# Casts of the line coordinates moved to ScalarE, the first tile's slots filled in parts, and a decoder layer's order of work chosen anew

## The chip, the cores and the metric

One core of a Trainium2 chip. The metric is the device time of one execution in microseconds (us). The engines are named as in the profile: PE (TensorE, matrix products), PEld (its weight loads), DVE (VectorE), ACT (ScalarE), POOL (GpSimd), SP (SyncE, which here only starts transfers).

## The reference

One decoder layer on x of 2048 tokens by 256, in float32:

1. `x = x + attn(layernorm(x))`. Self attention with 16 heads, causal, of an unusual kind. Of each token and head two 4-vectors `q1, q2` are made from the token and its predecessor, and two, `k1, k2`, from the token. Each pair becomes a line of 6 coordinates, `p1[i]*p2[j] - p1[j]*p2[i]` over the 6 pairs of indices, divided by its norm. Logits are products of the lines of queries and keys, times 6^-0.5.
2. `x = x + xattn(layernorm(x), ctx)`. Cross attention, 16 heads, over a context of 1601 rows.
3. `x = x + ffn(layernorm(x))`. 16 experts, 64 tokens each, chosen with 6 Sinkhorn rounds and a top-k, hidden width 1024.

## The kernel before

**Tiles.** The tokens are cut into 4 tiles of 512 (`NT`), each of 4 blocks of 128 (`BPT`). Self attention runs over query tiles, 4 groups of 4 heads, and key blocks up to the diagonal; cross attention over query tiles, groups and 13 context blocks. One block of one group is a *quad*: 160 of self attention and 208 of cross attention, 368 in all. A quad is two `scores` steps (products of keys and queries into one of two PSUM pairs, then one exponential on ACT, L1216, into `probs`; on the diagonal POOL then masks, L1076) and one `pv` step (the product with the values into `po`, L1824). At the end of a group ACT copies `po` out (L1228).

**Lines.** The 6 coordinates of a tile's queries and keys are made on DVE in steps `("lines", j, part)`. Part 0 (L1415 to L1421) makes the products, part 1 (L1425 to L1429 and `rsqrt`, L1280 to L1285) their difference and its inverse norm. Part 2 (L1438 to L1442) multiplies by it and cuts each float32 into three bfloat16 parts, so that bfloat16 products keep the precision:

```
l3 = l3 * rn
line_parts[0] = bf16(l2)                 # cast, L1439
t2 = l2 - line_parts[0]                  # L1440
line_parts[1] = bf16(t2)                 # cast, L1441
line_parts[2] = t2 - line_parts[1]       # L1442
```

For a product six combinations of the parts of a query and a key are stacked as six *slots*: `Q_SLOTS = (0, 1, 0, 1, 2, 0)`, `K_SLOTS = (0, 0, 1, 1, 0, 2)`. For tiles 1 to 3 the parts are turned by PE (`line_turn`, L1900), stored to DRAM and loaded into the slots by 24 transfers. The first tile takes a shorter way: `("slots", 0)` copies the parts into `slotted` with `copy_to_slots` (L839), the 12 copies of the queries on ACT and the 12 of the keys on DVE, both after L1442; then 8 `slot_turn` steps, each 8 transposes on PE (L1889) and a copy of the result by ACT (L1156) or DVE, fill `q_line` and `k_line`. The first scores (L1804) wait for all 8.

**Around them.** `prep` steps load and normalize the tokens (`stats` L1293, `norm` L1367, `x_turn` L1867) and `project` them (L1877, L1880; the result copied out at L1394 and L1396 by DVE, or L1151 and L1153 by ACT). `ctx_k` (L1852) and `ctx_v` (L1861) project the context, `join` adds an attention's result, `max` steps (L1932 on PE, L1509 on DVE: 64 for each of 16 tile-groups) find the largest cross logit of each token and head. A `shift` step and `shift_turn` (L1517 to L1529) turn the maxima of one tile-group into a row that is stored (L966), loaded (L972) and subtracted in the cross scores; without it the scores of that tile-group can't begin.

**The order.** Every engine is in order, and all take their instructions from one list, `PLAN`. `build_plan` makes it: ten streams of steps (`x`, `lines`, `ctx`, `keys`, `ones`, `max`, `query`, `weights`, `scores`, `pv`) are merged greedily. Each candidate step costs its idle time and start, and for each other stream the delay it causes there times a weight of that stream (table `W`). The durations and waits that the planner assumes stand in `work()`. The streams `lines`, `ctx` and `x` have weights of their own (`early_...`) until tile 1's lines are loaded. The weight of `max` is `W["max"]` while `max` steps lag behind `(pv steps done - max_from) / (368 - max_end - max_from)` of them, else `max_ahead`. The planner also chooses, for the kinds in `EITHER`, whether DVE or ACT copies a result out of PSUM; `act_early` and `act_late` are what ACT costs extra before and after the first scores.

## Time and profile before

| | us |
|---|---|
| median of 3 runs (lowest, highest) | 1152.06 (1151.38, 1155.24) |
| the profiled execution's own time | 1152.26 |
| its span | 1150.5 |
| PE busy | 1096.7 (95%) |
| DVE busy | 853.2 (74%) |
| ACT busy | 725.3 (63%) |
| POOL busy | 142.1 (12%) |

The span is what the profiler saw between the first and the last instruction; 1.76 us of the execution's own time lie around it. The granted PE clock is shown in tenths of full speed in the page's slices, and as a fraction in the table of stretches. Busy time of PE is modelled from pipelined records, so a PE at 95% is not at 95% of its peak; what counts below is where it is idle, and at which clock it works.

### The profile page before, as it was taken

How to read it: one execution, taken by the hardware profiler on the slowest of the kernel's cores; microseconds unless marked ns; L12 is line 12 of the kernel's file. 1: busy time of each engine (PE TensorE's matmuls, PEld its weight loads, DVE VectorE, ACT ScalarE, POOL GpSimd, SP SyncE). 2: the span in 40 equal slices, each digit the busy share in tenths (PEclk: the TensorE clock that was granted, in tenths of full speed). 3: DMA queues.
4: the chain of work that ended last, by engine and by line, in shares of the span. 5: the costliest groups of instructions: out<-in, count | busy, mean ns of one | idle time of the engine just before them, and what ended most of it. 6: DMA issues, size and time to landing. Idle time of an engine off the chain costs nothing.

```text
span 1150.5 us, 30375 instructions
## 1 busy us (share of the span) xinstructions
PE 1096.7 (95%) x12606; PEld 512.7 (45%) x12606; DVE 853.2 (74%) x1999; ACT 725.3 (63%) x838; POOL 142.1 (12%) x253
## 2 busy tenths in 40 slices
PE   4799999999999999999999999999999999888997
PEld 2444332333433334444455555555555553467554
DVE  6965676288889898789888889788888892258621
ACT  0646577887677776776776787678785778520111
POOL 3142314122111101000101000010000000000222
PEclk8899999999999999999999999999999999889999
DMA  5031037932100100103321200111102000088696
GB/s 177 27 82 55 24 108 127 177 59 69 44 30 2 47 16 16 53 19 87 121 70 59 94 19 23 53 48 31 30 10 73 21 17 3 19 296 217 185 349 180
DMA packets 79241, 90.24 MB, mean 78 GB/s; under 512 B 16016, under 2 KB 71632, under 8 KB 79104
## 3 DMA queue, kind: packets, MB, share of 16 engines
q1 hardware_dynamic: 73200, 79.91, 24.5%
q10 hardware_dynamic: 4368, 6.29, 1.7%
q0 software_dynamic: 1536, 2.10, 1.0%
q8 instruction: 100, 1.64, 0.6%
q14 instruction: 37, 0.30, 0.1%
HBM read 73.36 MB, written 14.91 MB: 77 GB/s over the span
## 4 chain that ended last, share of the span: by engine, by line
PE 84%; DVE 8%; ACT 3%; issue 3%; POOL 1%; DMA 0%; DVEq 0%; POOLq 0%; ACTq 0%
PE po L1824 25%; PE g L1932 17%; PE scores L1800 15%; PE scores L1804 6%; PE g L1917 3%; PE g L2029 2%; PE g L2053 2%; PE g L1877 2%; ACT probs L1216 2%; PE g L1907 2%; PE g L1867 1%; PE g L1923 1%; PE g L1911 1%; PE g L1852 1%; PE scores L2042 1%
## 5 line engine op out<-in xcount | busy, mean ns | idle before, releaser
L1216 ACT ACTIVATE probs<-scores 128x1024 f32<-128x1024 f32 (+2 forms) x736 | 675.3, 967 | 236.8 <-PE scores L1800 132.3
L1509 DVE TENSOR_REDUCE mx<-g 128x1 f32<-128x400 f32 (+1 forms) x1024 | 524.2, 567 | 74.0 <-PE g L1932 64.6
L1932 PE MATMUL g<-cross_region,even_region 96*32 96x400 bf16 (+1 forms) x4096 | 306.0, 336 | 0.4
L1800 PE MATMUL scores<-even_region,cross_region 99*32 99x512 bf16 (+1 forms) x3264 | 252.2, 379 | 2.5 <-ACT probs L1216 2.5
L1824 PE MATMUL po<-probs,cross_region 128*32 128x512 f32 (+1 forms) x1664 | 223.4, 594 | 0.8 <-ACT probs L1216 0.8
L1932 PEld LDWEIGHTS g<-cross_region,even_region 96*32 96x32 bf16 x4096 | 120.0, 95 | 196.6 <-DVE mx L1509 99.4
L1824 PE MATMUL po<-probs,self_region 128*32 128x512 f32 (+3 forms) x1280 | 151.3, 547 | 3.3 <-POOL probs L1076 3.0
L1800 PEld LDWEIGHTS scores<-even_region,cross_region 99*32 99x32 bf16 (+1 forms) x3264 | 96.5, 96 | 98.2 <-issue 43.2
L1804 PE MATMUL scores<-self_region 36*128 36x512 bf16 (+3 forms) x640 | 103.4, 358 | 6.2 <-ACT probs L1216 4.2
L1043 POOL TENSOR_TENSOR rstd<-mv,half 128x1 f32<-128x1 f32 x48 | 28.0, 584 | 529.5 <-DVE mv L1295 529.5
L1076 POOL TENSOR_SCALAR_AFFINE_SELECT probs<-probs 128x256 f32<-128x256 f32 x128 | 56.7, 449 | 231.8 <-ACT probs L1216 230.9
L1804 PEld LDWEIGHTS scores<-self_region 36*128 36x128 bf16 x640 | 25.7, 93 | 118.1 <-ACT probs L1216 82.5
L1824 PEld LDWEIGHTS po<-probs,cross_region 128*32 128x32 f32 (+1 forms) x1664 | 55.2, 110 | 25.7 <-ACT probs L1216 5.9
L1246 ACT ACTIVATE even_region<-scores 128x1024 f32<-128x1024 f32 x4 | 4.1, 1023 | 81.8 <-PE scores L2042 81.8
L1833 PE MATMUL scores<-xbo_sb,ident 128*128 128x256 f32 x186 | 47.3, 406 | 0.0
L1824 PEld LDWEIGHTS po<-probs,self_region 128*32 128x32 f32 x1280 | 31.6, 110 | 31.0 <-issue 15.3
L1483 DVE RECIPROCAL rsum<-g 128x16 f32<-128x16 f32 x32 | 8.2, 256 | 47.5 <-PE g L1907 47.3
L1867 PE MATMUL g<-ident,xn 128*128 128x128 f32 x96 | 21.5, 307 | 18.9 <-DVE xn L1367 18.7
L1833 PEld LDWEIGHTS scores<-xbo_sb,ident 128*128 128x128 f32 x186 | 36.6, 203 | 5.3 <-issue 0.3
L1877 PE MATMUL g<-wself_sb,xn_t 128*128 128x512 f32 x64 | 34.0, 658 | 0.0
L1494 DVE TENSOR_TENSOR xb<-g,xb 128x256 f32<-128x256 f32 x32 | 13.6, 424 | 24.3 <-PE g L1917 23.6
L1228 ACT COPY o_region<-po 128x512 f32<-128x512 f32 x32 | 18.8, 588 | 14.0 <-PE po L1824 14.0
(294 smaller groups left out, 863.8 us busy)
## 6 DMA issues: line engine op xcount, KB each, us to landing
cross_region<-in_w SPq DMA_DIRECT2D x16, 1024.0 KB, 12.7
even_region<-xq_d SPq DMA_DIRECT2D x192, 64.0 KB, 2.3
self_region<-in_w ACTq DMA_DIRECT2D x6, 1024.0 KB, 6.6
self_region<-in_w SPq DMA_DIRECT2D x6, 1024.0 KB, 14.6
cross_region<-xk_d SPq DMA_DIRECT2D x24, 200.1 KB, 8.8
xb<-in_x SPq DMA_DIRECT2D x32, 128.0 KB, 3.2
xb<-x_d SPq DMA_DIRECT2D x32, 128.0 KB, 2.3
probs<-in_w SPq DMA_DIRECT2D x4, 1024.0 KB, 12.6
```

Of the source, the lines that this page charges most:

```text
L1043: pool.tensor_tensor(rstd[:, u % 4:u % 4 + 1], mv[:, u % 4, 1:2], half[:, 0:1], ALU.pow).then_inc(rstd_ready, 1)
L1076: pool.affine_select(out=d, in_=d, compare_op=ALU.is_ge, fill=0.0, base=0, pattern=[[0, 2], [1, P]], channel_multiplier=-1).then_inc(mask_ ...
L1216: act.activation(probs[0:rows, s % 4, :, off:], ps[s % 2][0:rows, :, off:], ACT.Exp, scale=LSCALE if QUADS[n][0] == "self" else 1.0).then_ ...
L1509: dve.reduce_max(mx[:, k % 2, b, h, c:c + 1], g[:, 0:n_keys], AX_X).then_inc(g_free, 1)
L1800: mm = pe.matmul(ps[s % 2][c:c + n_keys, a, :], k_cross[0:NS * DH + 3, h, i * P + c:i * P + c + n_keys], rhs, start=True, stop=True)
L1804: mm = pe.matmul(ps[s % 2][0:rows, a, off:], lhs, rhs, start=True, stop=True)
L1824: mm = pe.matmul(po[32 * a:32 * a + 32, off:], v[0:rows, i, h * VW:h * VW + 32], probs[0:rows, s % 4, a % 2, off:], start=(i == 0), stop=e ...
L1833: pe.matmul(bank, ident[:, :], xbo_sb[:, :], start=True, stop=True)
L1867: mm = pe.transpose(g[:, k * P:(k + 1) * P], xn[:, norm_no[u] % 2, k * P:(k + 1) * P], ident[:, :])
L1877: pe.matmul(g[:, :], xn_t[:, k, c + 1:c + 1 + P], wself_sb[:, k, 0:512], start=(k == 0), stop=False)
L1917: mm = pe.matmul(g[:, 0:D], attn_t[:, k, :], (wo_sb if step[1] == "self" else wxo_sb)[:, k, :], start=(k == 0), stop=(k == DK - 1))
L1932: mm = pe.matmul(g[q:q + 32, 0:n_keys], q_max[k % 2][0:NS * DH, h, b * P + q:b * P + q + 32], k_cross[0:NS * DH, 4 * (k % 4) + h, start:st ...
```

## The change

It does three things.

1. **Casts.** Part 2 of `lines` becomes parts 2, 3 and 4. DVE multiplies and signals `lines_whole`; ACT makes the first cast and signals `lines_cast`; DVE subtracts (part 3); ACT makes the second cast; DVE subtracts the last time (part 4). The instructions of part 0 move into a helper, `line_products`, unchanged.
2. **Slots.** `copy_to_slots` takes the part that it is to copy. `("slots", 0)` and `("slots", 1)` copy the slots that hold part 0 and part 1 (3 and 2 of the six, 6 and 4 copies on either engine) as soon as ACT has cast them, `("slots", 2)` the last one (2 copies). On DVE the order is part 3, slots 0, part 4, slots 1, slots 2; on ACT cast, cast, slots 0, slots 1, slots 2.
3. **Order.** Fifteen weights of the planner are different, and its table of durations has the new steps, so the whole list is another.

```diff
-W = dict(hungry=0.2496, fed=0.0083, act_near=0.2255, max=0.1307, max_ahead=0.0147, max_from=72.59, max_end=10.0224,
-         prep=0.7203, x=0.2428, lines=0.1574, ctx=0.1821, keys=0.0826, early_ctx=0.1984, early_lines=7.9028,
-         early_x=0.84, ones=0.4536, query=0.3458, weights=0.0036, start=0.5141, late=0.9255, act_late=70.0,
+W = dict(hungry=0.2498, fed=0.0083, act_near=0.2255, max=0.4357, max_ahead=0.0147, max_from=72.59, max_end=3.5078,
+         prep=0.1816, x=0.2428, lines=0.1873, ctx=0.1393, keys=0.0688, early_ctx=0.8164, early_lines=3.9514,
+         early_x=1.372, ones=0.4083, query=1.1524, weights=0.005, start=0.7342, late=0.9255, act_late=35.7,
          act_early=0.0026)
...
-        line_steps += [("lines", j, part) for part in range(3)]
+        line_steps += [("lines", j, part) for part in range(4)]
         if j == 0:
-            line_steps += [("slots", j)] + [("slot_turn", b, side) for b in range(BPT) for side in range(2)]
+            line_steps += [("slots", 0), ("lines", 0, 4), ("slots", 1), ("slots", 2)]
+            line_steps += [("slot_turn", b, side) for b in range(BPT) for side in range(2)]
             continue
+        line_steps += [("lines", j, 4)]
...
-            return [("DVE", (3.7, 6.8, 5.0)[part], before, step, LAG)]
+            if part == 0:
...
+                return [("DVE", 3.6, before, step, LAG)]
+            if part == 1:
+                return [("DVE", 6.8, [("lines", j, 0)], step, LAG)]
+            if part == 4:
+                return [("DVE", 1.0, [("lines_cast", j, 3)], step, LAG)]
...
+            return [("DVE", 1.0, before, step, LAG), ("ACT", 0.75, [step], ("lines_cast", j, part), LAG)]
         if kind == "slots":
-            return [("ACT", 4.3, [("lines", 0, 2)], ("slots_q",), LAG), ("DVE", 2.7, [("lines", 0, 2)], step, LAG)]
+            part = step[1]
+            before = [("lines_cast", 0, part + 2) if part < 2 else ("lines", 0, 4)]
+            return [("ACT", 0.72 * (3 - part), before, ("slots_q", part), LAG),
+                    ("DVE", 0.45 * (3 - part), before, step, LAG)]
...
-        def copy_to_slots(copy, side):
+        def copy_to_slots(copy, side, which):
 
             for s, part in enumerate((Q_SLOTS, K_SLOTS)[side]):
+                if part != which:
+                    continue
...
# ScalarE
-                elif step == ("slots", 0):
-                    act.wait_ge(lines_split, 1)
-                    last = copy_to_slots(act.copy, 0)
-                    last.then_inc(slots_q, 1)
+                elif step[0] == "lines" and step[2] in (2, 3):
+                    _, j, part = step
+                    act.wait_ge(lines_whole, 2 * j + part - 1)
+                    src = (lines if part == 2 else lines_t).rearrange("p s h c -> p s (h c)")
+                    act.copy(line_parts[:, :, part - 2, :], src).then_inc(lines_cast, 1)
+                elif step[0] == "slots":
+                    if step[1] < 2:
+                        act.wait_ge(lines_cast, step[1] + 1)
+                        copy_to_slots(act.copy, 0, step[1])
+                    else:
+                        act.wait_ge(lines_split, 1)
+                        copy_to_slots(act.copy, 0, 2).then_inc(slots_q, 1)
...
# VectorE
-                        link(dve.tensor_tensor(l3, l3, line_rn.unsqueeze(2).broadcast_to((P, 8 * H, NC)), ALU.mult))
-                        link(dve.tensor_copy(line_parts[:, :, 0, :], l2))
-                        link(dve.tensor_tensor(t2, l2, line_parts[:, :, 0, :], ALU.subtract))
-                        link(dve.tensor_copy(line_parts[:, :, 1, :], t2))
+                        dve.tensor_tensor(l3, l3, line_rn.unsqueeze(2).broadcast_to((P, 8 * H, NC)),
+                                          ALU.mult).then_inc(lines_whole, 1)
+                    elif part == 3:
+                        dve.wait_ge(lines_whole, 2 * j + 1)
+                        dve.wait_ge(lines_cast, 2 * j + 1)
+                        dve.tensor_tensor(t2, l2, line_parts[:, :, 0, :], ALU.subtract).then_inc(lines_whole, 1)
+                    else:
+                        dve.wait_ge(lines_whole, 2 * j + 2)
+                        dve.wait_ge(lines_cast, 2 * j + 2)
                         dve.tensor_tensor(line_parts[:, :, 2, :], t2, line_parts[:, :, 1, :],
                                           ALU.subtract).then_inc(lines_split, 1)
                 elif kind == "slots":
-                    dve.wait_ge(lines_split, 1)
-                    copy_to_slots(dve.tensor_copy, 1).then_inc(slots_k, 1)
+                    if step[1] < 2:
+                        dve.wait_ge(lines_cast, step[1] + 1)
+                        copy_to_slots(dve.tensor_copy, 1, step[1])
+                    else:
+                        dve.wait_ge(lines_split, 1)
+                        copy_to_slots(dve.tensor_copy, 1, 2).then_inc(slots_k, 1)
```

## Rows read from the trace of the kernel before

**Rows 1.** The page's head, and its slices of PE busy and PE clock over the span
```profile
span 1150.5 us, 30375 instructions
...
PE   4799999999999999999999999999999999888997
PEclk8899999999999999999999999999999999889999
```

**Rows 2.** Busy time of each engine in stretches between events: us (instructions), clock, DMA share, GB/s
```profile
20.80:35.60 14.80, 7.91 (x22) 4.35 (x22) 13.93 (x49) 2.24 (x7) 2.49 (x4) 0.65 0.10 28
35.60:44.60 9.00, 7.35 (x27) 4.09 (x28) 7.41 (x22) 4.77 (x18) 0.00 (x0) 1.00 0.06 15
44.60:52.70 8.10, 5.18 (x68) 4.07 (x69) 7.79 (x29) 7.47 (x9) 1.09 (x2) 1.00 0.15 51
52.70:60.00 7.30, 6.07 (x32) 0.97 (x32) 6.75 (x17) 4.80 (x8) 3.18 (x6) 0.53 0.00 0
100.00:320.00 220.00, 213.10 (x1810) 77.01 (x1809) 148.15 (x348) 156.92 (x187) 50.68 (x93) 0.98 0.38 83
957.50:993.00 35.50, 31.85 (x407) 10.13 (x404) 1.02 (x4) 33.28 (x36) 0.00 (x0) 1.00 0.01 2
```

**Rows 3.** The timeline, 20 to 33 us: start, duration, engine, line, operation, idle before
```profile
24.38 0.43 DVE L1293 BATCH_NORM_STATS2 bn<-xb 128x6 f32<-128x256 f32 x1
26.64 0.66 PE L1867 MATMUL g<-ident,xn 128*128 128x128 f32 x2 [6.93 <-DVE xn L1367]
28.21 3.62 PE L1877 MATMUL g<-wself_sb,xn_t 128*128 128x512 f32 x4
32.67 1.88 PE L1877 MATMUL g<-wself_sb,xn_t 128*128 128x512 f32 x4
```

**Rows 4.** The timeline of VectorE, part 2 of the first tile's lines
```profile
35.65 0.95 DVE L1438 TENSOR_TENSOR even_region<-even_region 128x768 f32<-128x768 f32 x1
36.63 0.56 DVE L1439 CAST even_region<-even_region 128x768 bf16<-128x768 f32 x1
...
38.82 0.96 DVE L1442 TENSOR_TENSOR even_region<-even_region 128x768 bf16<-128x768 f32 x1
```

**Rows 5.** The timeline, first tile's slots, turns and first scores
```profile
39.89 1.54 DVE L839 COPY probs<-even_region 128x192 bf16<-128x192 bf16 x12
40.92 0.38 ACT L1153 COPY even_region<-g 128x256 f32<-128x256 f32 x1
41.18 3.13 ACT L839 COPY probs<-even_region 128x192 bf16<-128x192 bf16 x12
45.23 7.41 ACT L1156 COPY self_region<-g 100x1024 bf16<-100x1024 bf16 x8 [0.91 <-PE g L1889]
52.69 0.86 PE L1804 MATMUL scores<-self_region 36*128 36x512 bf16 x4 [1.39 <-ACT self_region L1156]
```

**Rows 6.** ScalarE's groups nearest to the new cast, from the page and from one line's durations
```profile
L1216 ACT ACTIVATE probs<-scores 128x1024 f32<-128x1024 f32 (+2 forms) x736 | 675.3, 967 | 236.8 <-PE scores L1800 132.3
L1228 ACT COPY o_region<-po 128x512 f32<-128x512 f32 x32 | 18.8, 588 | 14.0 <-PE po L1824 14.0
...
L1156 ACT COPY self_region<-g x8: 1012/1042/1077, 45.2 to 51.6; 100x1024 bf16<-100x1024 bf16 x8
```

**Rows 7.** The timeline around the last tile's second cast
```profile
182.23 1.43 POOL L1068 MEMSET cross_region<- 32x1604 f32 x1 [2.48 <-DMA xk_d<-cross_region]
182.31 1.77 DVE L1441 CAST even_region<-even_region 128x768 bf16<-128x768 f32 x1
184.38 0.42 PE L1824 MATMUL po<-probs,self_region 128*32 128x128 f32 x8 [1.67 <-POOL probs L1076]
```

**Rows 8.** The end of the maxima: their line, the last shift's load, the last group's first scores
```profile
L1509 DVE TENSOR_REDUCE mx<-g x28: 560/566/575, 939.5 to 956.0; 128x1 f32<-128x400 f32 x21, 128x1 f32<-128x401 f32 x7
...
960.25 0.25 SPq L972 DMA_DIRECT2D even_region<-shift_d  x1
965.74 0.61 PE L1800 MATMUL scores<-even_region,cross_region 99*32 99x512 bf16 x8
```

More of the change, by code:

```diff
@@ L285, in work @@
             b = step[1]
[L286 removed]
+            return [("PE", 0.5, [("lines", b // BPT, 4)] + bank, ("line_turn_pe", b), LAG),
                     (by, 0.8 if by == "ACT" else 0.57, [("line_turn_pe", b), ("line_stored", b - 4)], ("line_turn", b), LAG),
@@ L1430, in _ @@
                         rsqrt(line_rn, line_n2, flat_t[:, 0:P])
-                    else:
+                    elif part == 2:
                         if j == 1:
```

44 lines of the change are left out of this document (24 added, 20 removed).

## The prediction

> **What bounds the kernel now.** I first read the page's head and slices [rows 1]: PE is busy nine tenths or more nearly everywhere, and its clock is full except in a few slices. The whole is bound by PE, so a change gains only where PE is idle or at its lower clock. Then I cut the span at events [rows 2]. Four places are open. From 20.8 to 35.6 us PE works 7.91 of 14.80 us, at a clock of 0.65, while DVE is busy 13.93. From 44.6 to 52.7 PE works 5.18 of 8.10 while ACT is busy 7.47. From 52.7 to 60 PE works 6.07 of 7.30 at a clock of 0.53. From 100 to 320 it is idle 220.00 - 213.10 = 6.90 us. The fifth, 957.5 to 993, has ACT at 33.28 of 35.50: there the exponentials set the pace.
>
> Up to the first scores at 52.69 [rows 5] one chain matters: projections, lines on DVE, slots, turns. The timeline shows its end. DVE multiplies at 35.65, casts, subtracts, casts, subtracts until 38.82 + 0.96 = 39.78 [rows 4]. ACT, held until 41.30 by a copy of a projection, makes its 12 slot copies from 41.18 to 44.31; DVE's 12 take 1.54 and end at 41.43. Then ACT alone empties the eight turns, 7.41 us from 45.23 [rows 5]. What feeds PE other work in that time comes late: it is idle 6.93 us before the transposes at 26.64, since DVE makes part 0 of the lines and then, from 24.38, the statistics that the normalization waits for [rows 3].
>
> **The casts.** A cast of 768 elements takes DVE 0.56 [rows 4]. ACT's is not in the trace: a copy of 512 takes 0.588, one of 1024 two-byte elements 1.042 [rows 6]; midway is 0.81, and I take 0.80, with the two rows as bounds. Each cast also has two hand-offs. On DVE the first slot copy follows the last subtraction by 39.89 - 39.78 = 0.11, and ACT's copies of even 0.38 overlap, 41.18 being before 40.92 + 0.38 [rows 4, 5]; I take 0.05 for each. The pitch of DVE's cast is 0.60: from 36.63 to 38.82 lie two casts and a subtraction, and the multiplication, as long as a subtraction, has a pitch of 36.63 - 35.65 = 0.98 [rows 4], so (2.19 - 0.98) / 2. Part 2 then ends 2 x (0.80 + 0.10 - 0.60) = 0.6 later than 39.78, at 40.4.
>
> The Trainium skill has a rule against this, in "ScalarE: Activation LUTs", section "Rules for kernel authors": plain arithmetic belongs on VectorE, which is faster per element. Its own figure, 186 ns plus 0.833 per element, gives an estimate of 0.83 us for this cast, and so 0.06 more for the pair than my sum; the row of DVE agrees that VectorE is faster here.
>
> **The slots.** ACT's pitch is 3.13 / 12 = 0.26 [rows 5]. Its queue is cast, cast, then 6 + 4 copies from about 39.4, which end at 42.0, then the last 2, which wait for 40.4 only: 42.5, against 44.31. That is 1.8 earlier if no copy of a projection is in front, and 1.1 if a projection's two copies, of 0.38 each like the row's, still are. I take 1.3, bounds 0 and 1.8. On DVE the 6 + 4 + 2 copies end by 41.3 and don't matter.
>
> **The turns.** Eight turns cost ACT 7.41, PE only 5.18 in that stretch with all else [rows 2, 5]. Shared by DVE and ACT they could end 7.41 - 5.18 = 2.2 sooner. Weight `early_lines` halves, so DVE is less reserved for tile 1's lines, but nothing says that the planner shares them: 0.7, bounds 0 and 2.2.
>
> **The first hole.** `early_ctx` rises from 0.198 to 0.816, `early_x` from 0.84 to 1.372, and `early_lines` falls from 7.90 to 3.95. A delay of the lines was worth 40 of the context's and is now worth 5; so some context or token work should come before or between the parts of the lines, and enter PE's 6.93 us. It also delays the lines themselves. The four matrix products after the hole take 3.62 at the low clock, 1.88 later [rows 3], 1.7 more to have. Bounds 0 and 6.9 + 1.7 = 8.6. I take 2.3, near the lower end, because DVE, full at 13.93 of 14.80 [rows 2], is what context work needs too.
>
> **Later tiles.** ACT gets 6 more casts, 4.8 us, in stretches where it is busy 156.92 of 220 [rows 2], so they lie beside PE's work. DVE loses 6 x 0.6 = 3.6 us but now stands in its queue for each cast, behind at worst one exponential of 0.97 [rows 6] and with its own evacuations behind it, for which PE's three banks wait. Six times (0.97 + 0.30) = 7.6 of DVE, of which PE feels what its filler work doesn't cover: I take 0.7 lost, bounds 0 and 4.
>
> In the last tile the second cast took 1.77 instead of 0.56, overlapping a POOL memset, and PE then waited 1.67 for a mask behind it [rows 7]. With the cast on ACT, or the order another, this may go: I take 0.9 gained, bounds 0 and 1.67. The Trainium skill explains the row in "SBUF — State Buffer", section "SBUF: two separate sides": VectorE and GpSimd lock a pair of ports against each other and ScalarE has its own. By that rule an ACT cast is never held so.
>
> **Everything else** that the new order moves (weights `prep`, `query`, `ctx`, `keys`; the loads in SP's queue; the fills and masks in POOL's) goes at 0, bounds +4 and -3: it acts inside the 6.90 us idle of 100 to 320, and from 320 on PE is full [rows 1, 2]. Every instruction of PE stays, only its place changes.
>
> **Sum.** -1.3 - 0.7 - 2.3 + 0.7 - 0.9 = -4.5. The profiled execution took 1152.26, 0.20 above the median of 1152.06; so 1152.06 - 4.5 = 1147.6, call it 1147.5, which is 0.4% less. About 0.3%, 3.5 us, is what a measurement of this kernel can tell from no change: faster is below 1148.6, slower above 1155.5.
>
> **Rivals.**
>
> *The hole is filled.* Context work enters the first hole in earnest. For it: the weight ratio falls eightfold, and PE is idle there with ACT doing 2.24 of 14.80 us [rows 2]. Against: the context's cut needs DVE. Near the bounds, -1.8 - 2.2 - 6 - 1 = -11: 1141.
>
> *Given back.* First scores come earlier, but into the stretch where exponentials, masks and tile 1's lines already leave PE at a clock of 0.53 [rows 2]; an earlier start only lengthens it, as the next tile's lines are then what is late, now with two hand-offs more. For it: DVE is the fuller engine there, 6.75 of 7.30. Time 1152, or 1150 to 1154. That the change does not do what it says is part of this: the list may come out so that a projection's copies stand before the slots as now. The ScalarE page's rule of the Trainium skill points the same way.
>
> *The maxima come late* (slower). `max_end` falls from 10.02 to 3.51. When the last group of 13 quads is due, at pv 355, the wanted share is (355 - 72.59) / (368 - 72.59 - 3.51) = 0.967, before 0.990: of 1072 steps 35 may be undone, before 11. The 24 between would take DVE 24 x 0.566 = 13.6 us [rows 8]. Before, the last load of a shift was issued at 960.25, and the first scores of the last group ran at 965.74 [rows 8]: with some 2.3 for landing, as the planner takes it, 3.2 of slack. So it decides from 6 maxima more on, and at 24 costs 10.4: with the other terms 1152.1 - 4.5 + 10.4 = 1158. Against: the last maxima ran at 956.0 [rows 8], all done before the share asked for them, since PE takes them when ACT has work in store, and `max` weighs three times more when behind.
>
> **Chances.** The forecast's own case 0.38 (1143 to 1148.6), the filled hole 0.13, given back 0.31, maxima late 0.12, the waits for ACT's casts at their upper bound with nothing won 0.06. Faster 0.51, same 0.31, slower 0.18. The likeliest case alone has 1143 to 1150. The range reaches down to 1140, nearly all of the filled hole, and up to 1156, given back with its bounds and half of the slower cases.
>
> **What would show it.** Right: casts on ACT of 0.75 to 0.85; the last slot copy on ACT 0.5 to 0.7 after the last subtraction; first L1804 near 49 to 51; PE idle under 5 us before the second tile's transposes; the last tile's second cast under 1 us. Wrong: first scores at 52 or later; more idle of PE between 52 and 100 us than now; L1509 after 960 us, with PE idle in front of the last group; DVE idle behind casts on ACT for over 1 us each in 100 to 320 with PE idle beside it.

## The result, and the profile after

The kernel after the change took 1158.33 us in the median of 17 executions (1154.36 to 1163.03), the one before, run beside it on the same chips, 1151.58 (1147.93 to 1155.24, 17 executions). The ratio is 1.0058, 95% interval [1.0045, 1.0071]: 6.7 us slower, where 4.5 less was forecast, and above the range.

The page of the kernel after, its head and busy shares:

```profile
span 1155.2 us, 30383 instructions
...
PE 1096.9 (95%) x12606; PEld 512.8 (44%) x12606; DVE 850.1 (74%) x1992; ACT 729.6 (63%) x845; POOL 142.2 (12%) x253
```

PE is busy 1096.9 us, as much as before (1096.7), and the span is 1155.2 instead of 1150.5. So the 4.7 us that the profiled execution lost are idle PE; its busy time did not grow. The stretches say where (busy us of PE, PEld, DVE, ACT and POOL with their instructions, granted clock, DMA share, GB/s):

```profile
20.00:55.70 35.70, 26.23 (x136) 17.20 (x136) 31.13 (x102) 14.23 (x33) 4.69 (x8) 0.86 0.11 39
...
60.00:100.00 40.00, 36.16 (x265) 15.34 (x258) 29.94 (x68) 21.00 (x34) 17.67 (x34) 0.97 0.22 59
100.00:320.00 220.00, 211.99 (x1745) 76.13 (x1747) 134.55 (x321) 156.48 (x188) 47.85 (x91) 0.95 0.39 85
320.00:940.00 620.00, 616.74 (x8853) 285.23 (x8848) 537.03 (x1170) 462.21 (x494) 37.20 (x70) 1.00 0.15 43
...
80.00:100.00 20.00, 17.36 (x121) 7.34 (x120) 17.25 (x40) 8.88 (x15) 9.33 (x17) 1.00 0.27 75
...
160.00:180.00 20.00, 17.48 (x110) 4.44 (x110) 14.75 (x47) 13.31 (x18) 12.68 (x17) 0.74 0.91 118
```

The first row ends at the first scores, 55.70, which before came at 52.69 [rows 5]: 3.0 late. From 60 to 320 PE is idle 3.84 + 8.01 = 11.85 us. Before, it was 1.09 from 60 to 100 (busy 38.91) and 6.90 from 100 to 320 [rows 2], 7.99 in all; the clock of the longer stretch was 0.98 and is 0.95. From 320 to 940 there is 3.26 of idle PE, before 1.90 (busy 618.10), at a full clock in both. The twelfth group of heads ends at 296.57 us, before at 290.72: 5.9 late, more than the 4.8 at the end of the last group (998.87 and 994.08). So the time is lost ahead of 320 us, while the lines of the later tiles are made. The last two rows are the worst stretches of 20 us in there, with 2.64 and 2.52 of idle PE; before they had 0.13 and 0.06 (busy 19.87 and 19.94).

The first tile, in the timeline (start, duration, engine, line, operation, idle before and its releaser):

```profile
23.07 0.66 PE L1904 MATMUL g<-ident,xn 128*128 128x128 f32 x2 [3.56 <-DVE xn L1408]
...
37.36 0.95 DVE L1466 TENSOR_TENSOR even_region<-even_region 128x768 f32<-128x768 f32 x1
...
38.34 0.83 ACT L1238 CAST even_region<-even_region 128x768 bf16<-128x768 f32 x1 [1.60 <-DVE even_region L1466]
...
40.48 0.41 PE L1904 MATMUL g<-ident,xn 128*128 128x128 f32 x2 [3.56 <-DVE xn L1408]
...
41.23 0.83 ACT L1238 CAST even_region<-even_region 128x768 bf16<-128x768 f32 x1 [2.06 <-DVE even_region L1471]
...
42.24 3.15 ACT L855 COPY probs<-even_region 128x192 bf16<-128x192 bf16 x12
...
45.89 0.61 PE L1926 MATMUL g<-identb,probs 128*100 128x128 bf16 x8
...
48.48 2.30 PE L1926 MATMUL g<-identb,probs 128*100 128x128 bf16 x24 [1.99 <-DVE rest L1345]
...
52.93 1.89 DVE L1487 COPY self_region<-g 100x1024 bf16<-100x1024 bf16 x3
...
53.83 1.95 PE L1898 MATMUL g<-cross_region 128*128 128x256 f32 x8
...
55.70 0.60 PE L1841 MATMUL scores<-self_region 36*128 36x512 bf16 x4
```

Against [rows 3 to 5]: PE's one idle time of 6.93 has become two of 3.56, before different tokens' transposes. The casts on ACT take 0.83. From the multiplication to the last slot copy are 42.24 + 3.15 - 37.36 = 8.03 us, before 44.31 - 35.65 = 8.66 [rows 4, 5], so the slots did gain 0.6; but the multiplication is 1.7 later. The turns began at 45.89 and stopped for a context step (PE waits 1.99 for DVE's L1345, which frees a PSUM bank). DVE copied three of the eight results (L1487), and a context step (53.83 to 55.8) still stood ahead of the first scores.

The casts of ScalarE alone, from one line's view, and the last tile's second cast in the timeline:

```profile
L1238 ACT CAST even_region<-even_region x8: 822/832/855, 38.3 to 186.8; 128x768 bf16<-128x768 f32 x8
```

```profile
185.65 1.16 DVE L1471 TENSOR_TENSOR even_region<-even_region 128x768 f32<-128x768 f32 x1
...
186.84 0.83 ACT L1238 CAST even_region<-even_region 128x768 bf16<-128x768 f32 x1 [0.66 <-DVE even_region L1471]
```

Eight casts, 822 to 855 ns. In the last tile the cast starts 0.03 after the subtraction and takes 0.83, where DVE took 1.77 beside a memset of POOL [rows 7]; in this order no memset runs beside it. An exponential stands right behind it (187.58), but PE has a query projection to do until 187.9 and does not wait here. Nor do casts of the other tiles lie in the two worst stretches: they begin at 66.71, 69.88, 105.51 and 111.65, and ACT stood idle 0.62 ahead of the second and 2.29 ahead of the third. From this trace alone the casts look harmless, which the experiments contradict.

The end of the maxima, which one rival rested on:

```profile
L1546 DVE TENSOR_REDUCE mx<-g x1024: 552/565/578, 233.3 to 960.6; 128x1 f32<-128x401 f32 x86, 128x1 f32<-128x400 f32 x85
```

```profile
965.08 0.25 SPq L1005 DMA_DIRECT2D even_region<-shift_d  x1
...
970.54 0.61 PE L1837 MATMUL scores<-even_region,cross_region 99*32 99x512 bf16 x8
```

The last maxima begin at 960.6, the last shift's row is loaded from 965.08 and the last group's first scores run at 970.54: each 4.6 to 4.8 later than in [rows 8], and no more apart. The lateness is inherited.

### The profile page after: what moved, and what is told of

The parts are those of the page before. It is cut to its first block, busy times and chain, and to the rows that moved or that the text cites. A ratio compares the mean times of both kernels' runs of the same rounds, so it can differ in the third digit from the quotient of the medians.

```text
span 1155.2 us, 30383 instructions
## 1 busy us (share of the span) xinstructions
PE 1096.9 (95%) x12606; PEld 512.8 (44%) x12606; DVE 850.1 (74%) x1992; ACT 729.6 (63%) x845; POOL 142.2 (12%) x253
## 4 chain that ended last, share of the span: by engine, by line
PE 83%; DVE 8%; ACT 4%; issue 3%; POOL 1%; DMA 0%; DVEq 0%; POOLq 0%; ACTq 0%
PE po L1861 24%; PE g L1969 17%; PE scores L1837 15%; PE scores L1841 6%; ACT probs L1257 3%; PE g L1914 3%; PE g L1954 3%; PE g L2066 2%; PE g L2090 2%; PE g L1904 2%; PE g L1944 1%; PE scores L1870 1%; PE g L1960 1%; PE g L1948 1%; PE scores L2079 1%
## 5 line engine op out<-in xcount | busy, mean ns | idle before, releaser
L1969 PE MATMUL g<-cross_region,even_region 96*32 96x400 bf16 (+1 forms) x4096 | 309.7, 336 | 0.4
L1861 PEld LDWEIGHTS po<-probs,cross_region 128*32 128x32 f32 (+1 forms) x1664 | 55.8, 110 | 24.8 <-ACT probs L1257 4.6
```

Source lines behind the costliest of these rows:

```text
L1861: mm = pe.matmul(po[32 * a:32 * a + 32, off:], v[0:rows, i, h * VW:h * VW + 32], probs[0:rows, s % 4, a % 2, off:], start=(i == 0), stop=e ...
L1969: mm = pe.matmul(g[q:q + 32, 0:n_keys], q_max[k % 2][0:NS * DH, h, b * P + q:b * P + q + 32], k_cross[0:NS * DH, 4 * (k % 4) + h, start:st ...
```

## Experiments

Each text set off below was written before its run. Theory A, after this result: **the casts on ScalarE cost it**, through ACT's order (the second cast waits for DVE's subtraction, and exponentials queue behind). Rival B: **the new list costs it** (first scores 3 us late, turns interrupted). Rival C: both are small and the rest is the planner's luck: any list made anew lands some us away. Ratios are to the kernel before, run in the same job, with 95% intervals; a ratio of 0.001 is 1.15 us. Where an edit keeps a list (the order of work) and changes only code, this is said.

### Code against list

The list of the kernel before with the code of the change: `build_plan` as before, each old step replaced by the new ones in place.

```diff
+SPLIT = {("lines", j, 2): [("lines", j, 2), ("lines", j, 3), ("lines", j, 4)] for j in range(1, NT)}
+SPLIT["lines", 0, 2] = [("lines", 0, 2), ("lines", 0, 3), ("slots", 0), ("lines", 0, 4), ("slots", 1), ("slots", 2)]
+SPLIT["slots", 0] = []
...
-        plan.append(step)
+        plan += SPLIT.get(step, [step])
```

> The casts on ScalarE and the slots in parts, in the list of the kernel before: wherever that list had part 2 of the lines, it now has parts 2, 3 and 4 in a row, the first tile's with the slots between them; no other step moves. Theory 'order' (the new list loses the time, the casts don't): 0.997 to 1.001 of the kernel before, first scores 1 to 2 us earlier than 52.69. Theory 'hand-off' (VectorE waiting for ScalarE's casts holds PSUM banks, and PE with them): 1.003 to 1.006, with VectorE idle over 1 us in front of the subtractions of tiles 1 to 3 and PE idle beside it.

Measured: **1.0041 [1.0018, 1.0064]**, 1155.52 us. The new code alone, in the old order, costs most of the loss: theory 'hand-off' has its range, theory 'order' not. Its first scores come at 54.71, not earlier than 52.69: ACT's first cast stood behind a projection's copies, and DVE waited 3.37 us for it.

The changed kernel's list with both casts of every tile back on DVE:

```diff
-                        dve.tensor_tensor(l3, l3, line_rn.unsqueeze(2).broadcast_to((P, 8 * H, NC)),
-                                          ALU.mult).then_inc(lines_whole, 1)
+                        link(dve.tensor_tensor(l3, l3, line_rn.unsqueeze(2).broadcast_to((P, 8 * H, NC)), ALU.mult))
+                        dve.tensor_copy(line_parts[:, :, 0, :], l2).then_inc(lines_cast, 1)
```

> The changed kernel's list to the step, slots in parts too, but each cast made by VectorE inside its step, so that ScalarE has none of the 8. Theory 'order': 1.004 to 1.008 of the kernel before, as the changed kernel. Theory 'hand-off': 0.998 to 1.002, the loss is gone.

Measured: **1.0020 [1.0000, 1.0041]**, 1153.81 us, though its first scores come no earlier (56.17). So the casts are worth 0.0038 in this list (the two intervals don't meet), and the list about 0.002 without them. Its trace has the same two worst stretches, PE busy 17.98 from 80 to 100 and 17.84 from 160 to 180: these belong to the list and not to the casts. DVE is at 15.94 of 20 in the first of them, POOL at 12.99 in the second, before at 14.80 and 3.32.

The changed kernel with the weights of before, so a third list:

```diff
-W = dict(hungry=0.2498, ..., max=0.4357, ..., early_ctx=0.8164, early_lines=3.9514, early_x=1.372, ...
+W = dict(hungry=0.2496, ..., max=0.1307, ..., early_ctx=0.1984, early_lines=7.9028, early_x=0.84, ...
```

> The changed kernel with the fifteen weights of before; the planner has the new steps and makes a list of its own. Theory 'order', in the form that the weights are at fault: 0.998 to 1.003. Theory 'hand-off': 1.003 to 1.007. If any list that the planner makes is off by several us by chance, both are missed and it can lie anywhere in 0.997 to 1.008.

Measured: **1.0082 [1.0057, 1.0107]**, 1160.0 us, the slowest median of all (6 executions), with the first scores at 52.58. It is above the range of both theories; only the third, a list that is off by chance, reaches it. The weights of the change look better for the new steps than the old ones, but the intervals of 1.0058 and 1.0082 overlap. And the kernel before with the new weights (the same lines exchanged, in the kernel before), a fourth list:

> The kernel before with the fifteen new weights and nothing else. Theory 'order', weights at fault: 1.003 to 1.008. Theory 'hand-off': 0.998 to 1.002. With this and the run with the old weights the two factors, code and weights, stand crossed.

Measured: **1.0008 [0.9993, 1.0024]**, 1151.72 us. This one matters for how to read a trace. Its first group ends (ACT's copy of `po`) at 71.25 us, in the kernel before at 62.42; yet it isn't told apart from it. PE was busy 43.46 us of the first 60, before 38.4: the other work was done first. How early the first scores run says little about the end. Of the theories, A has 0.0038 of 0.0058 in one list and 0.0041 in the other; B has some 0.002; C is true of lists in general (1.0008, 1.0020 with DVE's casts, 1.0082), but doesn't explain a loss that appears with the list unchanged.

### Which tiles' casts, which part of the code

The changed kernel with ACT's casts in the first tile only, and in the later tiles only; the others' casts go back to DVE. The first of the two (the second has `step[1] > 0` and `j > 0`):

```diff
+                elif step[0] == "lines" and step[2] in (2, 3) and not (step[1] == 0):
+                    pass
...
+                        if not (j == 0):
+                            dve.wait_ge(lines_whole, 2 * j + 1)
+                            dve.tensor_copy(line_parts[:, :, 0, :], l2).then_inc(lines_cast, 1)
```

> The changed kernel's list, casts on ScalarE in the first tile only; tiles 1 to 3 cast on VectorE in the same step. With all casts on VectorE this list gave 1.002, with all on ScalarE 1.006. Theory 'later tiles' (VectorE waits for ScalarE among the exponentials): 1.001 to 1.003 here. Theory 'first tile' (the way to the first scores is what counts): 1.004 to 1.007.

> The mirror of the run before: casts on ScalarE in tiles 1 to 3, on VectorE in the first. Theory 'later tiles': 1.004 to 1.007. Theory 'first tile': 1.001 to 1.003. If the two runs both lie near 1.004, each part carries half.

Measured: 1.0065 [1.0045, 1.0085] and 1.0049 [1.0026, 1.0071]. They don't add up to the 1.0058 of both, from 1.0020 for neither: within the intervals either alone may cost as much as the two together. Theory 'later tiles' missed with the first of the two, theory 'first tile' with the second. In this list it stays open which tile's casts matter.

The traces don't settle it either. The last group ends at 997.27 us with all casts on DVE, 998.87 with all on ACT, 999.74 and 999.61 with a part of them there. What differs is the granted clock of the executions: 0.979 in the mean for the changed kernel's 17, 0.984 for the 12 with all casts on DVE. Within each of the two kernels 0.001 of clock goes with some 0.8 to 1.0 us, so these 0.005 are an estimate of 4 to 5 us, as much as the 0.0038. So in this list the price of the casts goes with PE's clock. That the casts lower it, by holes behind which the clock falls, fits the pair below, but isn't shown here.

The old list (`SPLIT` as in the first experiment), the slots in parts, all casts on DVE; and the same with the casts of tiles 1 to 3 on ACT. Between the two stands only

```diff
-                        if not (j > NT):
+                        if not (j > 0):
                             dve.wait_ge(lines_whole, 2 * j + 1)
```

and its like for the second cast and on ACT.

> The list of the kernel before, all casts on VectorE, only the first tile's slots in parts (part 3 between, the project copy and the carry after the slots). If this part of the change is worth what I gave it, ScalarE ends its slot copies 1 to 2 us earlier than 44.31, first scores come near 51, and the ratio is 0.997 to 1.000. If filling in parts is what loses (its copies stand in front of other steps): 1.002 or more.

> As the run before, with the casts of tiles 1 to 3 on ScalarE. Against that run it measures the hand-off in the later tiles alone, in the old list, in which VectorE's step was never planned with a wait: theory 'later tiles' 0.002 to 0.005 more than the run before; theory 'first tile' no more than 0.001 more, and then the 1.004 of the old list with all casts on ScalarE is owed to the first tile's cast, which stood 3.37 us behind two copies of a projection.

Measured: **0.9989 [0.9972, 1.0006]**, 1149.68 us, and **1.0048 [1.0030, 1.0067]**, 1156.98 us. Here is the clean pair: one list, six casts moved, 0.0059, a little more than theory 'later tiles' allowed. The ends of groups in the two traces are the same within 1.7 us up to the seventh (after the first, 1.5 apart; after the seventh, 1.6); the eighth ends at 185.75 in the one and at 191.34 in the other, the last at 995.18 and 1001.61. So 5.6 of 6.4 us are there by 191, and 4.0 of them came between the ends of the seventh group and the eighth, while the lines of tile 3 are cut. The timelines there, first with the casts on DVE:

```profile
181.80 1.99 PE L1962 MATMUL g<-xn_t,wxq_sb 128*128 128x512 f32 x4
...
183.46 1.49 DVE L1473 CAST even_region<-even_region 128x768 bf16<-128x768 f32 x1
...
185.26 0.43 PE L1863 MATMUL po<-probs,self_region 128*32 128x128 f32 x8 [1.47 <-POOL probs L1103]
```

and with them on ACT:

```profile
183.18 0.83 ACT L1234 CAST even_region<-even_region 128x768 bf16<-128x768 f32 x1 [1.69 <-DVE even_region L1462]
184.11 0.96 DVE L1470 TENSOR_TENSOR even_region<-even_region 128x768 f32<-128x768 f32 x1 [0.97 <-ACT even_region L1234]
...
185.11 0.83 ACT L1234 CAST even_region<-even_region 128x768 bf16<-128x768 f32 x1 [1.09 <-DVE even_region L1470]
185.84 0.65 ACT L1253 ACTIVATE probs<-scores 128x256 f32<-128x256 f32 x2
...
186.37 0.61 PE L1843 MATMUL scores<-self_region 36*128 36x512 bf16 x2 [3.08 <-ACT probs L1253]
...
186.91 3.78 PE L1962 MATMUL g<-xn_t,wxq_sb 128*128 128x512 f32 x4
...
191.34 0.59 ACT L1265 COPY o_region<-po 128x512 f32<-128x512 f32 x1 [3.30 <-PE po L1863]
```

This is the mechanism. ACT takes cast, cast, exponentials in this order. The second cast needs DVE's subtraction, so ACT stands 1.09 us, then casts for 0.83, and only at 185.84 come the two exponentials (L1253), though ACT stood idle at 184.0 with scores of 183.06 to take. PE waits 3.08 us for them. When it runs again the same four products of the query projection (L1962) take 3.78 instead of 1.99: the granted clock of that stretch is 0.50, of the stretch with 1.99 it is 1.00. The hole of 1.47 for a mask, which the first trace has, is not in the second, so the two differences 3.08 - 1.47 = 1.61 and 3.78 - 1.99 = 1.79 make 3.4 of the 4.0 us. The stretch of 180 to 200 us says the same (the two kernels, in this order):

```profile
180.00:200.00 20.00, 18.49 (x120) 5.53 (x123) 13.37 (x19) 13.52 (x17) 10.79 (x11) 0.91 0.88 167
```

```profile
180.00:200.00 20.00, 16.82 (x86) 5.09 (x82) 10.35 (x22) 10.02 (x15) 9.93 (x10) 0.74 0.62 94
```

Granted clock 0.91 and 0.74, PE busy 18.49 and 16.82. The casts of this tile are 1.7 us of ACT. What costs is what stands behind them and the clock afterwards. The first tile's casts add nothing here: with all eight on ACT the same list had 1.0041, with these six 1.0048.

### Is it ACT's order?

The old list with the casts of tiles 1 to 3 on ACT, tile 3's two moved down in the list, each behind an exponential, and the subtractions with them:

```diff
+SPACED = [(("cast", 3, 2), ("scores", 47, 0)), (("lines", 3, 3), ("cast", 3, 2)),
+          (("cast", 3, 3), ("scores", 47, 1)), (("lines", 3, 4), ("cast", 3, 3))]
...
+    for s, after in SPACED:
+        if s in plan:
+            plan.remove(s)
+        plan.insert(plan.index(after) + 1, s)
```

> The run with the old list and the casts of tiles 1 to 3 on ScalarE (1.0048), in which the last tile lost 5 us: there ScalarE's two casts stood in a row before the exponentials of quad 47, and the second waited 1.09 us for VectorE. Here the last tile's casts are steps of their own, each one exponential later, and so are the subtractions; nothing else moves. Theory 'queue' (the cast's wait holds the exponentials behind it, and they PE): PE's idle time before the scores of quad 48 falls from 3.08 to under 1.5 us, no 3.78 us query projections, and the ratio is 0.998 to 1.001. Theory 'hand-off' (VectorE's waits and the PSUM banks behind them, wherever the cast stands): 1.003 to 1.006.

Measured: **1.0012 [0.9996, 1.0029]**, 1153.77 us: of the 0.0059, 0.0036 gone; the two intervals, [0.9996, 1.0029] and [1.0030, 1.0067], don't meet, though barely. It lies just above theory 'queue' and below theory 'hand-off'. In its timeline

```profile
185.88 1.99 PE L1970 MATMUL g<-xn_t,wxq_sb 128*128 128x512 f32 x4
...
185.88 0.83 ACT L1242 CAST even_region<-even_region 128x768 bf16<-128x768 f32 x1 [1.45 <-DVE even_region L1470]
...
186.61 0.38 ACT L1261 ACTIVATE probs<-scores 128x256 f32<-128x256 f32 x1
...
190.01 0.43 PE L1871 MATMUL po<-probs,self_region 128*32 128x128 f32 x8 [2.14 <-POOL probs L1111]
```

an exponential (L1261) runs at 186.61, right after the first cast, and PE's query projection at 185.88 takes 1.99. The hole of 3.08 is gone; one of 2.14 behind a mask (L1111) stays, which the kernel with casts on DVE has too, at 1.47. (The forecast had said under 1.5.) DVE still waits for both of ACT's casts, 0.97 and 0.64 us, before 0.97 and 0.97; so it was not DVE's waiting that cost. Its profiled execution took 1159.54, well above its median, so its end is not read, but the distance over the place is: from the end of the seventh group to that of the ninth are 51.5 us, where the kernel without the spacing has 55.5 and the one with casts on DVE 50.8. A second look at that mask: `SPACED` as above in the old list, and only tile 3's casts on ACT:

```diff
-                        if not (j > NT):
+                        if not (j == 3):
```

> What the runs speak for, together: the list of the kernel before, slots in parts, casts on VectorE in tiles 0 to 2, the last tile's on ScalarE and each one exponential later, so that no memset of GpSimd can hold them. The slots in parts alone gave 0.9989 [0.9972, 1.0006]. If the 1.49 us cast and PE's 1.47 us wait in the last tile come back as gain: 0.997 to 0.999. If ScalarE's casts cost as much there as they save: 0.999 to 1.001.

Measured: 1.0006 [0.9993, 1.0020], 1153.5 us.

```profile
186.96 1.43 POOL L1103 MEMSET cross_region<- 32x1604 f32 x1 [2.35 <-DMA xk_d<-cross_region]
...
188.46 1.22 POOL L1111 TENSOR_SCALAR_AFFINE_SELECT probs<-probs 128x256 f32<-128x256 f32 x1
...
189.73 0.42 PE L1869 MATMUL po<-probs,self_region 128*32 128x128 f32 x8 [2.15 <-POOL probs L1111]
```

ACT's second cast, at 187.51, takes 0.83 beside this memset, and nothing is won by it: PE still waits 2.15 us for the mask. The mask stands behind the memset in POOL's own order, which ends at 186.96 + 1.43 = 188.39. It was so before too: the memset of [rows 7] ends at 183.66, the mask runs from 183.72, and PE goes on at 184.38. The cast was not in PE's way there. This disposes of my "last tile" term.

The same spacing in the changed kernel's own list, for tiles 1 to 3: the cast goes behind the first exponential that lies between the DVE steps around it.

```diff
+    for j in range(1, NT):
+        for part in (2, 3):
+            n, last = plan.index(("lines", j, part)), plan.index(("lines", j, part + 1))
+            exps = [k for k in range(n, last) if plan[k][0] == "scores"]
+            plan.insert(exps[0] + 1 if exps else last, ("cast", j, part))
```

> The changed kernel, its list kept, with ScalarE's casts of tiles 1 to 3 as steps of their own, each behind the next exponential of the list if one stands before the subtraction that needs it. Theory 'queue': ScalarE no longer idles 2.29 us in front of the third tile's first cast, and the ratio falls from 1.0058 to 1.002 to 1.004. Theory 'spread over the list' (no single place holds the loss of the changed kernel): 1.005 to 1.007.

Measured: 1.0042 [1.0020, 1.0064], 1159.04 us (1149.57 to 1163.05). Not told apart from the changed kernel's 1.0058, and between the two theories. In its trace ACT's waits for DVE in front of the six casts are gone but for one of 0.21 us, where the changed kernel had 0.62, 2.29 and 0.66; the time hardly follows. So these waits are not what this list loses most by. What explains the pair in the old list is not shown to explain the whole loss in the new one.

### Is it the hole, or the clock after it?

The old list with casts of tiles 1 to 3 on ACT, and seven products that no result uses put where PE stood idle (the trace shows each as two):

```diff
                 if kind == "scores":
+                    if step == ("scores", 48, 0):
+                        keep_busy(7, bank(("x_query", 0, 0))[:, 0:D])
                     scores(step[1], step[2])
```

> The same run with the hole left as it is, but seven needless products of 0.4 us each (128x256, into the PSUM bank of the next projection, which overwrites them) on PE in it. Nothing waits less; what changes is that PE is not idle. Theory 'clock' (half of the loss is the half clock after the hole, 3.78 in place of 1.99 us for each of two query projections): 1.001 to 1.003. Theory 'idle only': 1.005, unchanged or longer.

Measured: 1.0038 [1.0022, 1.0054], 1155.59 us.

```profile
183.04 3.29 PE L1872 MATMUL g<-xbo_sb,ident 128*128 128x256 f32 x14
...
186.58 1.99 PE L1964 MATMUL g<-xn_t,wxq_sb 128*128 128x512 f32 x4
...
190.09 1.99 PE L1964 MATMUL g<-xn_t,wxq_sb 128*128 128x512 f32 x4
```

The added products fill 3.29 us, and the projections take 1.99 each: the clock is full. In the profiled execution (1152.06, the shortest of its eight) the ninth group ends at 216.29, 4.0 before the kernel without them (220.32). But the ratio falls only from 1.0048 to 1.0038, within the intervals. It meets neither theory. So the mechanism is seen in the trace, its worth of 4 us is not confirmed by the times.

The same for the first hole, behind the fourth projection, in the old list with the slots in parts and the casts on DVE (28 needless products in the trace):

```diff
+                if step == ("project", 3):
+                    for _ in range(14):
+                        pe.matmul(ps[0][:, 0, 0:D], ident[:, :], wself_sb[:, 0, 0:D], start=True, stop=True)
```

> The old list with slots in parts (0.9989), and on PE, behind the first tile's last projection, 14 needless products of 0.4 us each (128x256) that fill most of the 6.93 us in which it waited. Nothing that others wait for is delayed by more than the last of them. Theory 'clock': the first product of the next projections runs at 0.47 a matrix instead of 0.9, no half clock before 43 us, and 0.5 to 2 us less: 0.997 to 0.999. Theory 'covered' (the way to the first scores is VectorE's, so PE's clock there buys nothing): 0.9985 to 1.0005.

Measured: 1.0016 [1.0006, 1.0025], 1152.36 us, above the 0.9989 of the kernel without them and above the range of both theories.

```profile
19.68 6.21 PE L1989 MATMUL scores<-wself_sb,ident 128*128 128x256 f32 x28
...
28.03 1.88 PE L1916 MATMUL g<-wself_sb,xn_t 128*128 128x512 f32 x4
...
35.91 0.51 PE L1906 MATMUL g<-ident,xn 128*128 128x128 f32 x2 [3.18 <-DVE xn L1404]
...
36.22 3.51 PE L1916 MATMUL g<-wself_sb,xn_t 128*128 128x512 f32 x4
...
40.75 3.15 ACT L849 COPY probs<-even_region 128x192 bf16<-128x192 bf16 x12
```

The projections after the hole take 1.88 instead of 3.62 [rows 3], and nothing is won. DVE's lines don't come earlier, so a new hole of 3.18 opens at 35.91, and now the projection behind that one runs at half clock (3.51). ACT's copies of its result come at 40.22, and the slot copies stand behind them: 40.75, where the kernel without the products has 39.28. The hole was moved, to a place where its clock did matter.

### The first tile's parts

The old list, the slots in parts, the first tile's casts on ACT and ahead of the projection's copies on ACT (and `if not (j == 0)` at DVE's casts):

```diff
+SPACED = [(("lines", 0, 2), ("x_turn", "prep", 7, 7)), (("lines", 0, 3), ("lines", 0, 2))]
```

> The list of the kernel before, slots in parts, only the first tile's casts on ScalarE, and these moved ahead of the copy of project 6, which they had stood behind for 3.37 us. Tests my term for the first tile: casts and parts together end the slots 1 to 2 us earlier than 44.31, first scores at 51 to 51.7, 0.997 to 0.999. If casts of 0.84 us and two hand-offs each eat the gain: first scores at 52 or later and no less than the 0.9989 of the same list with its casts on VectorE.

Measured: 1.0001 [0.9986, 1.0016], 1151.88 us. The gain that my term promised is missed, the other case holds.

```profile
13.93 2.35 PE L1922 MATMUL g<-wself_sb,xn_t 128*128 128x512 f32 x4
...
37.08 0.95 DVE L1468 TENSOR_TENSOR even_region<-even_region 128x768 f32<-128x768 f32 x1
...
39.99 0.83 ACT L1240 CAST even_region<-even_region 128x768 bf16<-128x768 f32 x1 [1.09 <-DVE even_region L1476]
...
41.26 3.14 ACT L855 COPY probs<-even_region 128x192 bf16<-128x192 bf16 x12
...
53.14 1.03 PE L1849 MATMUL scores<-self_region 36*128 36x512 bf16 x4 [1.39 <-ACT self_region L1189]
```

From the multiplication to the last slot copy are 41.26 + 3.14 - 37.08 = 7.32 us, 1.34 less than the 8.66 of before. In the same list with DVE's casts, the 0.9989, it is less again:

```profile
35.91 0.95 DVE L1462 TENSOR_TENSOR even_region<-even_region 128x768 f32<-128x768 f32 x1
...
39.28 3.15 ACT L849 COPY probs<-even_region 128x192 bf16<-128x192 bf16 x12
...
51.41 0.60 PE L1843 MATMUL scores<-self_region 36*128 36x512 bf16 x4 [1.39 <-ACT self_region L1183]
```

39.28 + 3.15 - 35.91 = 6.52. ACT's queue is the bound in the first of the two: the second cast until 40.82, the projection's copies, 12 slot copies of 0.26. By their start times the first scores of the two are at 53.14 and 51.41, but 1.17 of those 1.73 us were there at the multiplication and have nothing to do with the edit: the first line of the first fence is a projection of 2.35 us, where four products of this shape take 1.88 in [rows 3]'s last row. Why isn't shown: the granted clock of that stretch reads 1.00. The same opening instructions end, with DVE's last copy of a projection, at 20.70 before (20.28 + 0.42), 21.08 in the kernel with DVE's casts and 22.25 here, all three with the old list. So from one trace to another the first scores can't be compared to better than some 1.6 us, and distances are taken from the multiplication.

The changed kernel with the two context steps moved behind the turns, and the same with all casts on DVE:

```diff
+    for s in (("ctx_v", 0), ("ctx_k", 0, 1)):
+        plan.remove(s)
+        plan.insert(plan.index(("slot_turn", 3, 1)) + 1, s)
```

> The changed kernel with two context steps (the second projection of keys and the first of values) moved behind the eight slot turns, among which its list has them. PE's 1.99 us wait for a bank in the turns should go and first scores come at 52 to 54 instead of 55.70. If the time follows the first scores: 1.003 to 1.004. If the context work is only put off: 1.005 to 1.007, as the changed kernel.

> The changed kernel's list with the two context steps behind the turns (1.0033 with casts on ScalarE) and every cast on VectorE (1.0020 with the context steps in their place). If the two parts add: 0.998 to 1.001. If the list costs what it costs however these two are set: 1.001 to 1.004.

Measured: 1.0033 [1.0011, 1.0054], 1154.16 us, and 1.0022 [1.0004, 1.0040], 1154.11 us. The turns are no longer interrupted, but the two steps now stand between turns and scores, and from the multiplication to the first scores are 59.70 - 39.74 = 19.96 us in the first of the two, against 55.70 - 37.36 = 18.34 in the changed kernel. That is 1.6 us later (4.0 by the start times, but 2.4 of them were there at the multiplication), with a time that is not longer (if anything shorter). So the 1.0033, though in the range for "the time follows the first scores", doesn't speak for it. Moving them with DVE's casts changes nothing: 1.0020 and 1.0022. So the interrupted turns cost nothing that can be measured, and the 0.002 of the new list lies elsewhere. Set side by side, these two runs put the casts at 0.0011 in the new list, with intervals that overlap, where the first pair had 0.0038: what the casts cost there is not known to better than that.

## Why the prediction was wrong

Two steps failed. The prediction priced a later tile's cast by what DVE waits for, and not by what stands behind it in ACT's order: the term "later tiles", 0.7 with a bound of 4, measured 0.0059, 6.8 us, in the old list. And it took each us ahead of the first scores for a us of the whole, so the 4.3 us of the first tile's terms were counted as gain, of which the runs show next to none. In the changed kernel's own list the casts account for 0.0038 of the 0.0058; where in that list they cost it isn't shown. Of the signs named beforehand, the cast's 0.83 us and the last tile's cast under 1 us came true, and so did two of the wrong kind: first scores at 55.70, after 52, and more idle PE between 52 and 100 us (48 - 41.64 = 6.36, before 48 - 44.99 = 3.01).

**The casts, 0.6 inside the slots' term.** The duration was right: 0.83, within the 0.75 to 0.85 that I named. The hand-off was 0.03 us to ACT and 0.10 to 0.11 back to DVE, 0.14 for a cast where 0.10 was assumed. In the old list, with nothing ahead of them, multiplication to the end of part 2 took 37.08 to 41.88, 4.80, where [rows 4] have 35.65 to 39.78, 4.13: 0.67 more, as worked out.

**The slots, -1.3.** Right in size where nothing stood in front: 1.34 with the casts on ACT in the old list, 2.14 with them on DVE, 0.63 in the changed kernel. But the time hardly shows it: 1.0001 and 0.9989, with intervals that hold 1. The failed step is the one that took each us ahead of the first scores for a us of the whole; the kernel before with the new weights, whose first group ends 9 us later and whose time is the same within its interval, says it isn't one. And the two parts of the change work against each other: the slots in parts unload ACT's queue, the casts load it.

**The turns, -0.7.** They were shared, three of eight on DVE, as hoped, but broken up by a step that waits for a bank; from the first turn's copy (46.57) to the first scores are 9.1 us, before 52.69 - 45.23 = 7.5. I had taken the weights to say which way the list would go. They didn't say it.

**The first hole, -2.3.** The list did change there, but PE idles 3.56 twice. With most of the first hole filled with needless products there was no gain, though the projections behind it ran at full clock. DVE was on the path, not the projections at half clock, so their 1.7 us were not to be had; a new hole of 3.18 opened later. What real work in the hole is worth no run shows apart from the list.

**Later tiles, +0.7.** This is the step that turned the sign. I priced what DVE waits for ACT and PE only through DVE. The other side was left out: ACT, in order, waits for DVE's subtraction, and the exponentials queued behind it are what PE waits for. In the old list it was 6.4 us in the trace and 0.0059 in the ratio, over the upper bound of 4 that I had set. 4.0 of the 6.4 came in one group: a hole of 3.08 us in place of one of 1.47, and the projection at half clock after it, 1.8 longer. 1.6 were there before it, no more than traces of this list differ by in the opening. ACT was 71% busy from 100 to 320, and I took that as room; but at this place PE had nothing else to do before the exponentials that ACT held back. Spaced among the exponentials, the casts cost 0.0023 and not 0.0059.

**The last tile, -0.9.** The cast did fall from 1.77 to 0.83. The rule of the Trainium skill ("SBUF — State Buffer", section "SBUF: two separate sides") is that ScalarE isn't held by the ports that VectorE and GpSimd share; the trace agrees, with 0.83 beside a memset. But the reading of [rows 7] was wrong: the mask that PE waited for stood behind the memset in POOL's order and not behind the cast. With the cast out of the way, PE waited 2.15 us for the same mask.

**Everything else, 0.** With casts on DVE the new list is 1.0020 [1.0000, 1.0041], inside the bound of +4 (2.3 us), and its interval reaches 1. I had no way to see its sign.

**Rivals.** "The maxima come late" gave the right side and, with 1158, the measured time, both by luck: no wait appeared there. "The waits for ACT's casts at their upper bound with nothing won" was the nearest case and got 0.06; its bound of 4 was too low. The rule of the Trainium skill in "ScalarE: Activation LUTs", section "Rules for kernel authors", which puts plain arithmetic on VectorE, points to the result. The estimate from the page's figure was 0.83 for the cast, and the rows say 0.832. The price it speaks of, the longer instruction, is the small part (8 times 0.27 us); the larger one, in the old list, is the place in the queue.

**What stays open.** Why the spacing that took back 0.0036 in the old list took back 0.0016 in the new, if anything; whether the casts lower the clock in the new list, and where; why there the casts of the first tile alone and those of the others alone each seem to cost as much as both; where the 0.002 of the new list lies. The best version found is the old list with slots in parts and the casts on DVE, 1149.68 us, 0.9989 [0.9972, 1.0006]: not told apart from the kernel before.

## What to carry to other kernels

Before work is moved to an engine because it is "only 70% busy", look at what stands behind the moved instruction in that engine's order. If it waits for the engine that hands it its data, everything behind it waits too, and where that feeds the bound engine the price can be the whole wait plus the slower clock after it: here some 3.4 us for two casts of 0.83. And measure the parts of a change apart: here one part was worth little or nothing by itself (0.9989, not told apart from 1) and another cost 0.0059.

## What the runs showed of the hardware that I had not expected

Single executions of one kernel follow the granted clock. The changed kernel with the casts on DVE and the turns moved took 1150.68 us at a mean granted clock of 0.990 and 1157.54 at 0.978; the one with the casts behind exponentials 1149.57 at 0.990 and 1163.05 at 0.975. That is 0.6 and 0.9 us for each 0.001 of clock. One profiled execution is therefore no measure of 0.4%: the profile of the spaced casts took 1159.54, its median is 1153.77. Much of this lies in the feed-forward part at the end. After the last group the list is the same in all eighteen kernels, 25 steps, and yet this end takes 152.4 to 157.8 us in their traces: 152.5 and 153.0 in the two where the granted clock from 1002 to 1147 us is 1.00, 156.3 to 157.8 where it is 0.94 to 0.96. Both occur with the old list and with the new one. So two traces are better compared by the ends of their groups than by their spans. Holes of PE of 3.08 and 6.93 us were followed by products at a granted clock of 0.50 (3.78 for 1.99, 3.62 for 1.88). With needless products in them it was 1.00 (1.99, 1.88), and yet the whole gained 0.001, within the intervals, in one place and nothing in the other. In the opening, up to about 15 us, the same products take up to twice their time for a different length in each trace, though the granted clock reads 1.00 there; that alone moved what follows by up to 22.25 - 20.70 = 1.55 us.
